# A four-layer graph network on one core: two of thirteen units of destinations summed from gathered rows, and the first degree lookup moved behind the eighth piece

## The reference, cut to what matters

```
layer 0 (one sum):    agg = segment_sum(x[src], dst);  h = relu(relu((x + agg) @ W1.T + b1) @ W2.T + b2)
layer 1 (four sums):  with self loops added; h = relu(segment_sum((h @ W)[src] * norm, dst) + b), three times; a fourth without relu
layer 2 (one sum):    segment_sum(norm * ((x @ Wn + bn)[src] + efeat @ We + be), dst) + (h + resid) / degs
layer 3 (two sums):   mean over neighbours @ W_l.T + b_l + x @ W_r.T, twice, with a relu between
after each layer:     x = layernorm(x + layer(x))
```

## Time and profile before

| | us |
|---|---|
| median of 3 runs | 2732.22 |
| the profiled execution, its own time | 2729.3 |
| its span | 2727.5 |
| TensorE busy | 2580.1 (95%) |
| VectorE busy | 1488.3 (55%) |
| ScalarE busy | 613.4 (22%) |
| GpSimd busy | 156.5 (6%) |

### The profile page before, as it was taken

One profiled execution on the slowest core, in us unless ns is written; L12 is line 12 of the kernel. 1 busy time (PEld: TensorE's weight loads), 2 busy tenths in 40 slices (PEclk: granted clock), 3 DMA queues, 4 the chain that ended last, 5 costly groups with the idle time before them and its releaser, 6 DMA issues.

```text
span 2727.5 us, 42004 instructions
## 1 busy us (share of the span) xinstructions
PE 2580.1 (95%) x16397; PEld 1478.7 (54%) x16397; DVE 1488.3 (55%) x5515; ACT 613.4 (22%) x737; POOL 156.5 (6%) x113
## 2 busy tenths in 40 slices
PE   2879999957999999999999999999999999999998
PEld 0657666733555555556555555555555555555555
DVE  6999999867777666666656623333222221112222
ACT  2768888760000011111111100000000000000000
POOL 3000000002000011111111100000000200000000
PEclk9999999988999999999999999999999999999999
DMA  6225222225767655555555555454554454545554
GB/s 162 77 71 75 93 94 94 105 76 169 221 207 221 186 175 174 173 172 171 172 180 169 148 150 185 138 139 136 139 138 136 136 136 138 138 137 155 151 151 115
DMA packets 233638, 395.59 MB, mean 145 GB/s; under 512 B 42298, under 2 KB 214158, under 8 KB 229976
## 3 DMA queue, kind: packets, MB, share of 16 engines
q1 hardware_dynamic: 203728, 326.08, 42.0%
q10 hardware_dynamic: 28904, 64.79, 7.3%
q0 software_dynamic: 800, 1.94, 0.2%
HBM read 343.43 MB, written 49.32 MB: 144 GB/s over the span
## 4 chain that ended last, share of the span: by engine, by line
PE 77%; DVE 18%; DMA 1%; ACT 1%; DVEq 1%; issue 1%; SPq 0%; ACTq 0%; POOL 0%; POOLq 0%
PE PS L1575 71%; DVE S L899 8%; DVE S L898 6%; PE PS L1760 1%; DMA XN<-in_x_dram 1%; PE PS L1767 1%; PE PS L1768 1%; PE PS L1782 1%; DMA HR<-adjacency 0%; PE PS L1765 0%; PE PS L1791 0%; PE PS L1764 0%; PE PS L1714 0%; PE PS L1740 0%; ACT XN L1391 0%
## 5 line engine op out<-in xcount | busy, mean ns | idle before, releaser
L1575 PE MATMUL PS<-HR,HN 128*128 128x500 fp8e3 (+1 forms) x5096 | 1061.3, 366 | 2.4 <-issue 1.9
L1575 PE MATMUL PS<-HR,AGN 128*128 128x500 fp8e3 (+1 forms) x4606 | 926.1, 350 | 3.2 <-DMA HR<-adjacency 3.1
L1575 PEld LDWEIGHTS PS<-HR,HN 128*128 128x128 f16 x5096 | 489.8, 97 | 517.2 <-issue 5.7
L1575 PEld LDWEIGHTS PS<-HR,AGN 128*128 128x128 f16 x4606 | 445.0, 97 | 391.1 <-issue 6.1
L1575 PE MATMUL PS<-S 128*128 128x245 f16 x1250 | 336.5, 276 | 43.1 <-DVE S L899 38.7
L899 DVE TENSOR_SCALAR S<-S,RBW 128x245 f16<-128x245 f16 x1250 | 341.5, 273 | 0.0
L1081 DVE TENSOR_SCALAR AT<-PS,SC 128x384 f32<-128x384 f32 (+24 forms) x100 | 43.2, 472 | 513.1 <-PE PS L1575 496.4
L898 DVE TENSOR_SCALAR S<-iot,RBW 128x128 f16<-128x128 f16 x1250 | 297.4, 238 | 2.3 <-PE PS L1575 1.7
L1575 PEld LDWEIGHTS PS<-S 128*128 128x128 f16 x1250 | 120.0, 97 | 166.7 <-issue 40.5
L1230 DVE TENSOR_SCALAR TB<-iot,dstF 128x208 f16<-128x208 f16 x833 | 159.1, 270 | 5.9
L677 POOL TENSOR_TENSOR AT<-AT,dstI 128x1088 f32<-128x1088 f32 x49 | 100.6, 2053 | 827.1 <-DVE mxe L1204 827.1
(11 more groups left out here) (241 smaller groups left out, 1821.6 us busy)
## 6 DMA issues: line engine op xcount, KB each, us to landing
HR<-adjacency SPq DMA_DIRECT2D x588, 437.5 KB, 3.5
AT<-source_lanes ACTq DMA_DIRECT2D x49, 544.0 KB, 5.2
AT<-in_edge_attr_dram ACTq DMA_DIRECT2D x48, 544.0 KB, 4.6
adjacency<-HN SPq DMA_DIRECT2D x9, 1531.2 KB, 5.5
adjacency<-HR SPq DMA_DIRECT2D x8, 1531.2 KB, 5.7
adjacency<-TB SPq DMA_DIRECT2D x8, 1531.2 KB, 5.6
HR<-adjacency SPq DMA_DIRECT2D x49, 218.8 KB, 2.5
edge_rows<-AT ACTq DMA_DIRECT2D x8, 416.0 KB, 12.6
```

Source lines behind the costliest of these rows:

```text
L1575: return t_.matmul(out_, w, m, start=start, stop=True, skip_group_check=True)
```

## The change

1. **Two units gathered.** Units 5 and 10 (`GU`, four subs, 1000 destinations) are no longer built as dense columns: the first stage makes 21 subs (`DSUB`) and 1050 windows. Their edges, sorted by destination, are cut in 8 blocks of 125 destinations (`GD`), each of 18 tiles of 128 edge slots (`GT`), 144 tiles in all. For each tile GpSimd gathers the 128 source rows, high and low half side by side (256 fp16 values, 512 B), from a copy of the rows in DRAM (`Xd`); VectorE makes the tile's one-hot of 128 slots by 125 destinations (`tile_hot`, `batch_hot`); TensorE multiplies them (125 weights, 256 columns) into one PSUM area per block; VectorE adds the two halves (`block_kept`, `block_read`); TensorE transposes the block back into the unit's place and adds the self term (`pair_turned`, `gathered_unit`).
2. **The passes** have 11 dense units, 77 pieces. The tiles are multiplied in 48 batches of three behind the pieces in `BATCH` (9 to 60). GpSimd issues a batch's gathers five pieces ahead in its own order, and VectorE its one-hots three ahead. The ring holds six batches (`GR`). A block's first product waits until VectorE has read the block before. Unit 5 ends 4 pieces after unit 4, unit 10 after unit 9.
3. **The halves** lie interleaved by block (`HLR`), so that a row's 256 values are contiguous. SyncE stores each part of them to `Xd` as soon as its low half is written, in its queue of slot loads; the gathers of a pass wait for all stores (`stored`).
4. **The lookups** run from piece 8 on: `LP = [PIECES + 1 + g * (PCS - PIECES - 6) // (NG - 1)]`.
5. **GpSimd's order** is one list with the pieces: the gathers, the 49 multiplications (each at the piece before an edge group), the first seven bias additions at the end of pass 1 instead of its start, the second seven at the end of pass 6. VectorE's edge maximum comes one piece earlier.
6. **The first stage** also decodes two more columns of edge slots (`decode_tiles`), gathers and multiplies the 144 tiles of the first sum in bursts of 18 (`block_sums`, in subs `BURST`), and checks that the gathered blocks hold every edge of their destinations (`fl` columns 6 and 7). Window buffers, zeros and window sums have moved to other memory; the semaphores of the general path are shared by two passes.

```diff
+    GU = (5, 10)
+    GD = SD_ // 2
+    GT = 18
+    NGB = 2 * len(GSUB)
+    NTL = NGB * GT
+    GB0, GB1, GR = 6, 3, 6
+    BURST = [4 + 4 * k // 3 for k in range(NGB)]
-    PCS = NU * PIECES
+    DU = [u for u in range(NU) if u not in GU]
+    PCS = len(DU) * PIECES
+        BATCH = [9 + b * 53 // NB1 for b in range(NB1)]
-        LP = [1 + g * (PCS - 6) // (NG - 1) for g in range(NG)]
+        LP = [PIECES + 1 + g * (PCS - PIECES - 6) // (NG - 1) for g in range(NG)]
...
                 for n in range(ALL):                       # SyncE
+                    if RING <= n < RING + NQ:
+                        q = n - RING
+                        sp.wait_ge(s_split, NQ + q + 1)
+                        sp.dma_start(rows(Xd[1])[:, q * QB:(q + 1) * QB, :], HLR[1][:, q * QB:(q + 1) * QB, :]).then_inc(s_xr[1], 16)
+                    for p_, u in DUE["low"].get(n - RING, ()):
+                        b0, b1 = blocks(u)
+                        sp.wait_ge(s_split, splits(p_, u))
+                        k = (p_ + 1) % 2
+                        sp.dma_start(rows(Xd[k])[:, b0:b1, :], HLR[k][:, b0:b1, :]).then_inc(s_xr[k], 16)
                     sp.wait_ge(s_af[m], slot_turns(m) * (p - 1) + i // RING + 1)
...
+            def tiles_of(p, b):                            # GpSimd
+                done = NB1 * (p - 1) + b - GR + 1
+                if done > 0:
+                    pool.wait_ge(s_gf, NB0 + done)
+                for k in range(GB1 * b, GB1 * (b + 1)):
+                    g_.indirect_dma_start(out=GR1[k % (GR * GB1)], out_offset=None, in_=Xd[p % 2][:, :],
+                                          in_offset=bass.IndirectOffsetOnAxis(ap=SI[:, k:k + 1], axis=0)).then_inc(s_gt[b % GR], 16)
...
-                bias_1()
-                pool.wait_ge(s_ns, 1)
-                for g in range(NG):
-                    weighted(g)
-                bias_5()
+                for n in range(ALL):
+                    p, i = n // PCS + 1, n % PCS
+                    if i == 4:
+                        pool.wait_ge(s_xr[p % 2], stored(p))
+                    for b in range(NB1):
+                        if BATCH[b] == i + 5:
+                            tiles_of(p, b)
+                    if n == PCS + 1:
+                        pool.wait_ge(s_ns, 1)
+                        weighted(0)
+                    if n == EP[0] - 2:
+                        weighted(1)
+                    if n + 1 in EDGES_AT and EDGES_AT[n + 1] + 1 in range(2, NG):
+                        weighted(EDGES_AT[n + 1] + 1)
+                    if n == PCS - 1:
+                        bias_1()
+                    if n == 6 * PCS - 1:
+                        bias_5()
...
+            def batch_hot(p, b):                           # VectorE
+                for m in range(GB1 * b, GB1 * (b + 1)):
+                    done = NTL * (p - 1) + m - 4 * GB1
+                    if done >= 0:
+                        dve.wait_ge(s_gf, NB0 + done // GB1 + 1)
+                    v.tensor_scalar(OH1[m % (4 * GB1)], iotC[:, 0:GD], DR[:, m:m + 1], UNIT, ALU.is_equal, ALU.mult).then_inc(s_goh, 1)
+            def block_read(p, k):
+                y = 512 * GBANK[p]
+                dve.wait_ge(s_gf, NB0 + NB1 * (p - 1) + GT // GB1 * (k + 1))
+                ...
+                v.tensor_reduce(SG1[k % 4], PS[0:GD, y:y + 2 * P].rearrange("p (h f) -> p f h", h=2), axis=AX, op=ALU.add).then_inc(s_sg, 1)
...
+            def tile_batch(p, b):                          # TensorE
+                k, e = divmod(b, GT // GB1)
+                y = PS[0:GD, 512 * GBANK[p]:512 * GBANK[p] + 2 * P]
+                ...
+                if e == 0:
+                    pe.wait_ge(s_sg, NGB * p + k)
+                pe.wait_ge(s_gt[b % GR], 16 * (GB0 * (NB0 // GR) + GB1 * (NB1 // GR * (p - 1) + b // GR + 1)))
+                pe.wait_ge(s_goh, NTL * p + GB1 * (b + 1))
+                for m in range(GB1 * b, GB1 * (b + 1)):
+                    last = mm(y, OH1[m % (4 * GB1)], GR1[m % (GR * GB1)], start=m % GT == 0)
+                last.then_inc(s_gf, 1)
```

429 lines of the change are left out of this document (326 added, 103 removed).

## The result

| | before | after |
|---|---|---|
| median, us | 2731.68 (4 runs, 2731.03 to 2732.32) | 2990.04 (4 runs, 2987.78 to 2992.43) |
| ratio | | 1.0946, 95% interval 1.0927 to 1.0965 |
| the profiled execution, its span | 2729.3, 2727.5 | 2987.8, 2986.0 |
| TensorE busy | 2580.1 (95%) | 2509.7 (84%) |
| VectorE busy | 1488.3 (55%) | 1723.6 (58%) |

What follows compares the result with a forecast made beforehand. VectorE was taken to bound the first stage, TensorE the passes, and VectorE pass 1 after the change. Terms -29 - 26 - 9 - 13 - 87 = -164 took the median 2732.2 to 2568 us, range 2515 to 2650.

Steps and rivals of the forecast that it cites:

- are hidden: First stage: the 144 gathers need 180 us of some 400 and so cost nothing.
- keep nearly all: Passes 4 to 7: gathers fit by 5%, 3 us given back each, so -21.7 us a pass, -87 together.
- about 0.02 us a gather: Passes: how much gathers disturb VectorE, read from eight window pairs taking 2.91 us beside eight gathers, 2.85 undisturbed.
- D: Rival: gathers set the pace of the passes; at 1.78 us a gather +206 us, 2938 us; chance 0.09.
- gathers stretched beside a full VectorE: By the skill's port rule, the 1.25 us a gather would stretch where VectorE is full, above all in the first stage.
- First stage: 200 of 1250 windows go, -71 us; VectorE's added work +37, TensorE's bursts +5; net -29 (bounds -45 and -10).
- Pass 1: The 23.7 us stand at the first lookup goes, VectorE becomes the bound: ends at 912 against 938.5, -26 us.
- the block read: Pass 1: eight block reads at 0.41 us each, 3 us of VectorE's 276.
- some 10 us: Pass 1: what GpSimd's seven bias additions (16.7 us) stretched VectorE by before; they now fall among lookups.
- +16 and +12: Passes 2 and 3: lateness because GpSimd needs 12.15 us per 12.0 us edge group; leaves -9 and -13 us.
- nothing, but 1 to 3 us a pass: Passes: cost of half-row stores ahead of slot loads on SP's queue; the larger figure if VectorE lags two pieces.
- rival C: Passes: the tile's weight load is not hidden, 15.4 us a pass, +108 over seven, 2676 us; chance 0.04.

Runs made afterwards that it cites:

- chip C: The changed kernel itself, unaltered, run again on another chip: 2673.11 us, ratio 0.9791 to the kernel before.
- m6: Fourth kernel of phases, its own kernel on chip E: engines alone or beside 40 gathers, with none to eight one-column fills between gathers; 877.13 us.
- m1: First kernel of phases, its own kernel on chip A: 160 one-hot pairs, alone or in a ring, beside gathers, loads or GpSimd work; 1119.37 us.
- part 2: The kernel before with one part of the change alone, the first lookup behind the eighth piece: 2710.46 us against 2731.42, ratio 0.9927.
- a2: The changed kernel without the 1008 gathers of the passes (rows are zeros), everything else kept, on chip A: 2773.52 us.
- v2: The changed kernel with a piece free of tile products between blocks and half-row stores one piece later, on chip D: 2906.40 us, ratio 1.0643.
- m5: Third kernel of phases, its own kernel on chip B: engines alone or beside 40 gathers, in a row or with drains and fills; 857.87 us.

## Why the prediction was wrong

Pass lengths, start to start, and the first stage to its last products (us):

| | stage 1 | p1 | p2 | p3 | p4 | p5 | p6 | p7 |
|---|---|---|---|---|---|---|---|---|
| before | 536.5 | 341.1 | 320.4 | 318.7 | 284.7 | 287.5 | 286.5 | 281.3 |
| forecast, difference | -29 | -26 | -9 | -13 | -21.7 | -21.7 | -21.7 | -21.7 |
| chip C, difference | -28.2 | +12.2 | +10.0 | +6.4 | -13.3 | -17.2 | -4.7 | -17.7 |
| the result, difference | +100.9 | +36.8 | +23.3 | +24.9 | +18.8 | +23.2 | +21.3 | +9.4 |

(The differences of stage 1 are those of pass 1's start; the turn between them kept its 61 us, as forecast.) Between the profiled executions (2987.8, chip C 2677.0, forecast 2729.3 - 164 = 2565.3) the miss of 422 us is 311 between the result and the same kernel on chip C, which I put down to the standing (129 in the first stage, 182 in the passes), and 112 between chip C and the forecast.

**The step that failed: the gathers "are hidden" (first stage) and "keep nearly all" (passes).** The prediction asked whether GpSimd would be fast enough, and it was: 1.25 us. It asked what gathers do to VectorE by eight gathers, and of those only the first 2.9 us: "about 0.02 us a gather". On a chip with the standing the same gathers, each 1.25 us, made VectorE's pairs come every 3.5 us instead of 0.356 and cost 129 us in the first stage alone. In the kernel after, the standing began with about the 17th gather of the first burst of 36, and in the later bursts of 18 with the fourth to ninth. The trace of before has eight in a row at most. It could not have shown the standing on any chip: the ten gathers of edge slots stand in the kernel after as well, and beside them VectorE did the same number of operations from gather to gather in the result as on chip C. It should have widened the range: the prediction took an effect seen over eight events for 1152. The rival that named the other side, D, had the right sign and nearly the right size (2938) by a wrong mechanism: in the result TensorE waited for a landing once, 2.0 us, so the gathers did not set the pace. That the number is near is luck.

The Trainium skill (SBUF — State Buffer, Who interferes with whom) has as its single rule that only the port pair shared by VectorE and GpSimd causes contention. The standing is not covered by it: in m6 TensorE and ScalarE stood beside GpSimd's gathers with VectorE idle, and VectorE's operations kept their length (0.29 us beside gathers) and only started late. Whoever takes the rule for the whole of what gathers do to other engines is wrong here; the measurement decides. What the prediction drew from the page, gathers stretched beside a full VectorE, showed only beside float32 one-hots (1.81 us in m1); beside the float16 ones of this kernel they kept 1.25.

**First stage otherwise right.** -28.2 on chip C, 46 to 508 us with VectorE at 449.9 of 462: -29 in the forecast.

**Pass 1: -26 forecast, +12.2 on chip C.** The first lookup's 23.7 us did go (part 2). The step that failed is the block read, priced at 0.41 us of VectorE and nothing for TensorE in this pass; TensorE waited 33.2 us for block reads in it. The read stands in VectorE's queue behind lookups of 4.14 us, and TensorE's next block behind it. The waits of TensorE in the kernel after on chip C, over the whole run (total, times, longest; L1461 is the block read):

```profile
PE PS L1815 <- DVE S L1461: 39.7, 19, 5.6
PE PS L1815 <- DVE HR L1461: 31.0, 6, 17.6
PE PS L1815 <- DMA HR<-adjacency: 30.0, 15, 4.2
```

and of the result:

```profile
PE PS L1815 <- DVE HR L1461: 47.0, 12, 17.7
PE PS L1815 <- DVE S L1461: 41.7, 15, 6.3
```

The longest stands behind the bias addition, moved to the end of pass 1 (timeline, chip C; a one-hot that takes 0.16 us elsewhere takes 14.92):

```profile
822.88 14.92 DVE L1452 TENSOR_SCALAR S<-S,DR 128x125 f16<-128x125 f16 x1
823.51 14.22 POOL L747 TENSOR_TENSOR XN<-XN,BR 128x896 f32 x7
...
842.27 0.42 DVE L1461 TENSOR_REDUCE HR<-PS 125x128 f32<-125x256 f32 x1
842.74 0.90 PE L1815 MATMUL PS<-HR,S 128*125 128x256 f16 x3 [17.57 <-DVE HR L1461]
```

I had priced it at "some 10 us" of VectorE, not as a block for TensorE. Here the same section of the Trainium skill is borne out: one holds the pair, the other "fully blocks". It speaks of one instruction; here the one-hot was held through all seven.

**Passes 2 and 3: +10.0 and +6.4, forecast -9 and -13.** Three block reads each, 3.6 to 5.6 us late, and the first slots. The step that failed is the +16 and +12 put down to GpSimd's "12.15 of 12.0". Without that lateness the forecast was -24.7 in each. In a2, without gathers, the two took 320.4 and 317.6 us: nothing is gained there either, so GpSimd's queue is not the reason for more than 17 us of both.

**Passes 4 to 7: -13.3, -17.2, -4.7 and -17.7, forecast -21.7.** TensorE's busy time was right (264.2 us in pass 4, where 284.8 - 24.7 = 260). The mis-sized term is SP's queue, "nothing, but 1 to 3 us a pass": TensorE waited 18.5 us for slots in these four passes, 0.6 before, because the first loads of a pass stand behind stores that wait for VectorE's last low halves (in v2, with the stores a piece later among its moves, the wait for slots was 19.9 us in all against the result's 29.4). Pass 6 lost another 7.2 us at its second rows.

**The 112 us together.** Block reads and slots are 70.7 + 30.0 - 3.3 (the wait for slots before) = 97 us of waiting, of the size of the 112. It is no full account, since the forecast had itself given back 28 us in passes 2 and 3 and 12 in passes 4 to 7. How much of it is not the gathers' doing, a2 shows: its seven passes, without any gather, took 2062 us together, where chip C took 2096 and the forecast says 1985. So 77 us of the miss come from the rest of the change, and 34 with the gathers on a chip without the standing. That waits for block reads go by order alone was shown by v2, on a chip with the standing only; on one without it v2 was not run.

**Right:** the tile's weight load is hidden (rival C: the tile products came 0.109 us apart, forecast 0.110, though a load of 125 weights took 0.137 us where the prediction's estimate was 0.104 and loads of 128 took 0.097; TensorE's busy time in passes 4 and 5, 264.2 and 264.0 us, is 4 and 1 above the forecast's 260.1 and 262.8, not 15); the general path was not taken; the landings were not waited for.

**Open.** What the late service is. Only its conditions are shown: gathers 1.25 to 1.50 us apart, five or more in a row (more, where fewer engines are at work), whatever their rows' size or number; in the result and in three of six groups of runs. In the passes gathers come in threes 1.25 us apart with pauses, 1.51 to 1.75 us on average, and each pass of the result was still 13 to 40 us longer than chip C's; what spacing a pass would need was not found. All runs were recorded for a profile, and whether the recording takes part can't be told from them. Whether it belongs to the chip for good wasn't seen either: no chip with it came twice, chip B was twice without.

## What to carry to other kernels

An operation that the old trace shows a few times is not priced for a thousand in a row: the number in a row, and who else runs beside it, belong to the price, and where the trace has no such stretch, the range has to say so. Give gathers space (here 2.19 us from one to the next did no harm to a first stage that 1.25 had made 120 us longer), and look at a change on more than one chip before believing its sign: here it is 9.5% slower on one and 2.1% faster on another, while its one-line part, the later lookup, gave 0.7% without needing any gather. A short read at the end of a block is priced by the longest operation ahead of it in its engine's queue, not by its own 0.41 us.

## What the runs showed of the hardware

- On three chips, 40 gathers in a row made VectorE, TensorE and ScalarE start late, from the fifth or sixth gather on with all three at work and from the 14th to 17th with VectorE alone: 16 of its operations in 20 us for 105. The same phases ran undisturbed on chip B (m5), the same kernel on chip C.
- TensorE's granted clock goes with it: 0.50 (1.2 GHz) in the windows where the full ring stood, 1.00 (2.4 GHz) in the phases alone and, in the window shown, in the standing ring of TensorE and ScalarE. It comes back late: m6's last gather of the phase without fills is at 327.1 us, the ring was full again from 336, and only from 340 on did TensorE do 41 instructions in 4 us instead of 23.

```profile
336.00:340.00 4.00, 4.00 (x23) 2.95 (x22) 4.00 (x24) 2.29 (x3) 0.00 (x0) 0.54 0.01 2
340.00:344.00 4.00, 4.00 (x41) 3.69 (x39) 4.00 (x24) 2.83 (x4) 0.00 (x0) 1.00 0.00 0
```

- Beside the ring with float32 one-hots the gathers came 1.44 us apart on chip B and 1.81 on chip A, beside float16 ones 1.25 on both.
- GpSimd's seven additions held a float16 one-hot of VectorE for 14.92 us, through all seven.
- A drain behind a gather waits for its landing: 3.36 us from gather to gather in m5, the next one issued 0.8 to 1.1 us after the landing.
